# Gates of the last experts copied to 64 rows by transfers, and a second PSUM bank for the gate product

## What is computed

```
scores = sigmoid(x @ gate_w.T)
...
w_dense = zeros((T, E)).at[arange(T)[:, None], tidx].add(tw)      # E = 64 gates for each token
def body(acc, ws):
    wg, wu, wdn, cw = ws
    hmid = silu(x @ wg) * (x @ wu)                                # F = 64
    return (acc + cw[:, None] * (hmid @ wdn), None)
y, _ = scan(body, zeros_like(x), (We_gate, We_up, We_down, w_dense.T))
shared = silu(hidden_states @ Ws_gate) * (hidden_states @ Ws_up) @ Ws_down
return y + shared
```

## Time and profile before

| | |
|---|---|
| median of 3 runs | 2336.13 us (2328.97 to 2339.03) |
| the profiled execution, its time | 2336.96 us |
| its span, first to last instruction | 2334.4 us |
| TensorE matmul busy | 2067.9 us (89%) |
| VectorE busy | 1549.5 us (66%) |
| ScalarE busy | 1335.2 us (57%) |
| mean granted clock of TensorE | 0.934 |
| DMA, mean over the span | 27 GB/s |

### The profile page before, as it was taken

How to read it: one execution, slowest core, us unless ns; L and a number is a source line. 1 busy time by engine, 2 the same in 40 slices (tenths; PEclk the granted TensorE clock), 3 DMA queues, 4 the chain that set the end, 5 groups by cost and what they waited for, 6 DMA issues and landing times.

```text
span 2334.4 us, 39953 instructions
## 1 busy us (share of the span) xinstructions
PE 2067.9 (89%) x14352; PEld 1061.6 (45%) x14352; DVE 1549.5 (66%) x3792; ACT 1335.2 (57%) x2644; POOL 265.0 (11%) x355
## 2 busy tenths in 40 slices
PE   7999988799989958888888888889888888878898
PEld 3444455545556723444444444444443444434433
DVE  6767577566757776766676666667676666764554
ACT  4666644367753324676676757667675766754311
POOL 0000000144430021011010101111110101010000
PEclk9999999799999957999999989889998989979999
DMA  4000000311020010010100101010001001030000
GB/s 162 1 1 1 1 1 1 129 40 42 37 67 3 15 34 24 6 29 8 41 12 19 37 13 29 4 46 12 19 21 28 25 5 29 2 113 1 1 1 9
DMA packets 64819, 62.16 MB, mean 27 GB/s; under 512 B 8401, under 2 KB 57714, under 8 KB 63218
## 3 DMA queue, kind: packets, MB, share of 16 engines
q1 hardware_dynamic: 64626, 59.62, 8.2%
HBM read 31.28 MB, written 0.52 MB: 14 GB/s over the span
## 4 chain that ended last, share of the span: by engine, by line
PE 44%; ACT 10%; DVE 6%; issue 4%; DMA 1%; SPq 1%; ACTq 0%; DVEq 0%
PE ps L1987 7%; PE ps L1967 6%; PE ps L1947 4%; ACT big L2498 4%; PE ps L2037 3%; ACT big L2579 2%; PE ps L2139 2%; PE ps L2123 2%; DVE C_nm L2686 2%; PE ps L2239 2%; PE ps L2260 2%; PE ps L2235 2%; PE ps L1996 2%; PE ps L2160 2%; PE ps L2149 1%
## 5 line engine op out<-in xcount | busy, mean ns | idle before, releaser
L2686 DVE TENSOR_REDUCE C_nm<-ps 128x1 f32<-128x512 f32 x768 | 498.7, 684 | 216.1 <-PE ps L1947 211.8
L2498 ACT ACTIVATE big<-ps 128x512 f32<-128x512 f32 x768 | 427.3, 596 | 216.4 <-PE ps L1967 209.0
L1947 PE MATMUL ps<-C_attn 62*128 62x512 bf16 x768 | 248.1, 412 | 64.2 <-DVE C_nm L2686 48.0
L1967 PE MATMUL ps<-C_attn 64*128 64x256 bf16 x1536 | 235.7, 293 | 51.5 <-ACT big L2498 35.1
L1987 PE MATMUL ps<-big,C_attn 128*32 128x256 f32 x3072 | 227.1, 417 | 19.3 <-ACT big L2498 18.2
L1967 PEld LDWEIGHTS ps<-C_attn 64*128 64x128 bf16 x1536 | 68.5, 96 | 226.2 <-ACT big L2498 99.9
L2579 ACT ACTIVATE big<-ps,C_biasx 77x512 f32<-77x512 f32 x192 | 115.6, 679 | 68.3 <-PE ps L2127 68.2
L1947 PEld LDWEIGHTS ps<-C_attn 62*128 62x128 bf16 x768 | 60.4, 95 | 181.6 <-DVE C_nm L2686 106.1
L2432 POOL TENSOR_SCALAR lnv<-mv 128x2 f32<-128x2 f32 x72 | 16.0, 222 | 1050.1 <-DVE mv L2668 1050.1
L1987 PEld LDWEIGHTS ps<-big,C_attn 128*32 128x32 f32 x3072 | 84.5, 115 | 109.1 <-issue 46.4
L2777 DVE TENSOR_REDUCE C_nmx<-ps 128x4 f32<-128x308 f32 x192 | 78.4, 470 | 57.6 <-PE ps L2101 56.8
(11 more groups left out here) (373 smaller groups left out, 4021.7 us busy)
## 6 DMA issues: line engine op xcount, KB each, us to landing
C_attn<-C_first SPq DMA_DIRECT2D x288, 64.0 KB, 2.1
B_rot<-B_rot SPq DMA_DIRECT2D x64, 128.0 KB, 2.0
C_w<-in_C_w SPq DMA_DIRECT2D x6, 1090.0 KB, 6.0
C_attn<-in_D_ew SPq DMA_DIRECT2D x4, 1536.0 KB, 9.9
big<-in_B_ew SPq DMA_DIRECT2D x8, 514.0 KB, 9.3
normw_later<-in_norm_w SPq DMA_DIRECT2D x1, 2304.0 KB, 16.8
A_w<-in_A_w SPq DMA_DIRECT2D x2, 1024.0 KB, 9.9
A_w<-in_A_w SPq DMA_DIRECT2D x2, 768.0 KB, 11.0
```

The costliest lines, as they stand in the source:

```text
L1947: pe.matmul(ps[:, bank, :], lhsT=qs[side(hp, MAX_ROW), b, hq, t * P:(t + 1) * P], rhs=ks[side(hp, MAX_ROW), b, hq, :], start=True, stop=Tr ...
L1967: last = pe.matmul(ps[:, bank, cols(pq)], lhsT=ks[side(1 - hp, HALF), b, hq, kt * P:(kt + 1) * P], rhs=qs[side(1 - hp, HALF), b, hq, cols( ...
L2498: act.activation(prob[:, kt % 2, q2, 1 - hp, :], ps[:, bank, :], ACT.Exp, scale=SCALE)\
L2686: dve.tensor_reduce(nm[:, group % 2, t % TH, hq % 4, hp:hp + 1], ps[:, bank, :], AX.X, ALU.max, negate=True).then_inc(emptied[bank], 1)
```

## The change

The gates are no longer split and multiplied by a selector. `take_gates` copies the turned gates, 64 rows of float32, from PSUM to `d.gT` in one operation. SyncE then issues, for every pair, a transfer that reads two rows of `d.gT` and writes each 64 times, into one of three buffers of 128x512 (two in `first`, one in `hT[0]`); VectorE's second multiply reads that buffer. Transfer `j` waits for the multiply of pair `j - 3`. The second half of the weights comes in four pieces (`LATE_D`) between these transfers. The freed PSUM bank 4 becomes a second bank for the gate product.

```diff
+LATE_D = 4
...
-        for half in range(2):
-            plan["DVE"].append((at + 114 + 14 * ROUTE_PARTS + 28 * half, "split_gates", b, half))
+        plan["DVE"].append((at + 114 + 14 * ROUTE_PARTS, "take_gates", b, 0))
...
-    d.gT = flat[0:96, 2 * S:4 * S].bitcast(BF16).rearrange("p (h b s) -> p h b s", h=2, b=B)
-    d.sel = flat[0:96, 4 * S:6 * S].bitcast(BF16).rearrange("p (e d) -> p e d", d=P)
+    d.gT = flat[0:E_D, 2 * S:4 * S].rearrange("p (b s) -> p b s", b=B)
+    d.spread = flat[:, 4 * S:6 * S].rearrange("p (i s) -> p i s", i=2)
...
+        spread = (d.spread[:, 0, :], d.spread[:, 1, :], hT[0][:, :])
...
-        GATE_BANK, UP_BANK, WB_BANK, DOWN_BANK = 2, 3, PV_BANK, 1
+        GATE_BANKS, UP_BANK, DOWN_BANK = (2, PV_BANK), 3, 1
...
-                    if k:
-                        pe.wait_ge(silu_done, k)
-                    pe.matmul(ps[0:rows_d(e), GATE_BANK, :], lhsT=gate, rhs=d.hT[:, b, :], start=True, stop=True)\
+                    if k == 1:
+                        pe.wait_ge(cw_ready, UNITS * QUADS)
+                    if k >= 2:
+                        pe.wait_ge(silu_done, k - 1)
+                    pe.matmul(ps[0:rows_d(e), GATE_BANKS[k % 2], :], lhsT=gate, rhs=d.hT[:, b, :], start=True, stop=True)\
...
-                        pe.wait_ge(h_ready, k)
-                        half, pair = divmod(e - 1, PAIR_D // 2)
-                        pe.matmul(ps[:, WB_BANK, :], lhsT=d.sel[:, pair, :], rhs=d.gT[:, half, b, :],
-                                  start=True, stop=True).then_inc(wb_done, 1)
...
+                sp.wait_ge(pv_done, UNITS * 16)
+                for j in range(B * PAIR_D):
+                    b, pair = divmod(j, PAIR_D)
+                    if pair == 0:
+                        sp.wait_ge(gT_ready, b + 1)
+                    if j >= 3:
+                        before, e = divmod(j - 3, PAIR_D)
+                        sp.wait_ge(h_ready, before * STEPS_D + e + 2)
+                    sp.dma_start(spread[j % 3], d.gT[2 * pair:2 * pair + 2, b:b + 1, :].broadcast_to([2, F_D, S]))\
+                        .then_inc(spread_landed[j % 3], 16)
+                    if 2 <= j < 2 * LATE_D + 2 and j % 2 == 0:
+                        i, step_d = j // 2 - 1, PAIR_D // 2 // LATE_D
+                        part = slice(PAIR_D // 2 + i * step_d, PAIR_D // 2 + (i + 1) * step_d)
                         sp.dma_start(ew[:, part, :, :], a["D_ew"][part].rearrange("e p k d -> p e k d"))\
-                            .then_inc(d_w_loaded[b], 16)
+                            .then_inc(late_loaded[i], 16)
...
+                def take_gates(b):
                     bank = arrived(dve, ("dw", b))
...
+                    dve.tensor_copy(d.gT[:, b, :], ps[0:E_D, bank, :]).then_inc(emptied[bank], 1)
+                    drained(dve, ("dw", b))
+                    dve.sem_inc(gT_ready, 1)
...
-                            dve.wait_ge(wb_done, b * PAIR_D + e)
-                            dve.tensor_tensor(eh[:, k % 2, :], emid[:, k % 2, :], ps[:, WB_BANK, :], ALU.mult)\
+                            j = b * PAIR_D + e - 1
+                            dve.wait_ge(spread_landed[j % 3], 16 * (j // 3 + 1))
+                            dve.tensor_tensor(eh[:, k % 2, :], emid[:, k % 2, :], spread[j % 3], ALU.mult)\
                                 .then_inc(h_ready, 1)
```

More of the change, by code:

```diff
@@ L1866, in stage_c @@
         w_loaded = (w_loaded0, w_loaded1)
-        (d_small, d_w_loaded0, d_w_loaded1, dn_ready, d_order, w_ready, gT_ready, sel_set, dsel_made, gate_done, up_done,
-         wb_done, silu_done, mid_done, h_ready, down_done, acc_ready) = \
+        (d_small, d_w_loaded0, dn_ready, d_order, w_ready, gT_ready, gate_done, up_done, silu_done, mid_done, h_ready, down_done, acc_ready) = \
             (m.sem("D_" + n) for n in
-             ("small", "w_loaded0", "w_loaded1", "dn_ready", "order", "w_ready", "gT_ready", "sel_set", "sel_made",
-              "gate_done", "up_done", "wb_done", "silu_done", "mid_done", "h_ready", "down_done", "acc_ready"))
-        d_w_loaded = (d_w_loaded0, d_w_loaded1)
+             ("small", "w_loaded0", "dn_ready", "order", "w_ready", "gT_ready",
+              "gate_done", "up_done", "silu_done", "mid_done", "h_ready", "down_done", "acc_ready"))
+        late_loaded = [m.sem(f"D_late_loaded{i}") for i in range(LATE_D)]
+        spread_landed = [m.sem(f"D_spread_landed{i}") for i in range(3)]
+        spread = (d.spread[:, 0, :], d.spread[:, 1, :], hT[0][:, :])
         y_added, with_eps = m.sem("C_y_added"), m.sem("C_with_eps")
@@ L2228, in enter @@
                         drained(pe, ("dl", b))
-                    if b == 0 and e in (1, 1 + PAIR_D // 2):
-                        pe.wait_ge(d_w_loaded[e // (PAIR_D // 2)], 32)
+                    if b == 0 and e == 1:
+                        pe.wait_ge(d_w_loaded0, 32)
+                    for i in range(LATE_D):
+                        if b == 0 and e == 1 + PAIR_D // 2 + i * PAIR_D // 2 // LATE_D:
+                            pe.wait_ge(late_loaded[i], 16)
                     if e == 0:
                         drained(pe, ("dn", b))
-                    if k:
-                        pe.wait_ge(silu_done, k)
-                    pe.matmul(ps[0:rows_d(e), GATE_BANK, :], lhsT=gate, rhs=d.hT[:, b, :], start=True, stop=True)\
+                    if k == 1:
[3 more added lines that the diff above has]
+                    pe.matmul(ps[0:rows_d(e), GATE_BANKS[k % 2], :], lhsT=gate, rhs=d.hT[:, b, :], start=True, stop=True)\
                         .then_inc(gate_done, 1)
@@ L2408, in _ @@
                 sp.dma_start(d.gb, a["D_gb"].rearrange("(o e) -> o e", o=1).broadcast_to([P, E_D])).then_inc(d_small, 16)
[L2409 to L2412, removed]
+                sp.wait_ge(pv_done, (UNITS - 1) * 16)
+                for i in range(2):
+                    part = slice(i * PAIR_D // 4, (i + 1) * PAIR_D // 4)
+                    sp.dma_start(ew[:, part, :, :], a["D_ew"][part].rearrange("e p k d -> p e k d"))\
+                        .then_inc(d_w_loaded0, 16)
+                sp.wait_ge(pv_done, UNITS * 16)
[11 more added lines that the diff above has]
+                        part = slice(PAIR_D // 2 + i * step_d, PAIR_D // 2 + (i + 1) * step_d)
                         sp.dma_start(ew[:, part, :, :], a["D_ew"][part].rearrange("e p k d -> p e k d"))\
-                            .then_inc(d_w_loaded[b], 16)
+                            .then_inc(late_loaded[i], 16)
             @block.gpsimd
@@ L2469, in spread_heads @@
                             .then_inc(sel_made, 1)
[L2471 to L2481, removed]
                 for _, n, s in timeline(GPSIMD):
-                    if n == UNITS - 1 and s in GPSIMD[n % B]["VX"]:
-                        spread_gates()
                     step(n, s)
@@ L2868, in route @@
                         dve.tensor_scalar(d.wd, d.wd, 2.5, None, ALU.mult).then_inc(w_ready, 1)
-                def split_gates(b, half):
+                def take_gates(b):
                     bank = arrived(dve, ("dw", b))
[L2872 to L2880, removed]
-                    cd.after(dve.tensor_copy(gT[32:64, :], d.rem[0:32, :]))
-                    cd.after(dve.tensor_copy(d.rem[32:64, :], d.rem[0:32, :]))
-                    ins = dve.tensor_tensor(gT[64:96, :], d.rem[32:64, :], gT[32:64, :], ALU.subtract)
-                    if half == 0:
-                        cd.after(ins)
-                    else:
-                        ins.then_inc(gT_ready, 1)
+                    dve.tensor_copy(d.gT[:, b, :], ps[0:E_D, bank, :]).then_inc(emptied[bank], 1)
+                    drained(dve, ("dw", b))
+                    dve.sem_inc(gT_ready, 1)
                 def expert(k):
```

17 lines of the change are left out of this document (4 added, 13 removed).

## The result

The changed kernel takes **2641.93 us** (median of four runs, 2621.76 to 2654.95) beside 2333.35 us for the kernel before on the same chip: 1.1313 times as long, 95% interval 1.1236 to 1.139. Forecast were 2784 us and 2460 to 2840 us. Direction and cause were right; the mean time of a transfer was set too high.

The account below looks back on a forecast made before the run. TensorE bound the second batch before; afterwards the transfers would. Gates ready at 2088.1, first packet 2089.6, 64 x 10.5 = 672.0, weights 8.6, tail 10.8: span 2781.0, plus 2.6 around it, 2784 us; range 2460 to 2840 us.

Parts of the forecast that it names:

- krow's 16 KB: Earlier transfer, two neighbouring SBUF rows each copied to 8 places: 0.65 us, 25 GB/s, taken as model for gate transfers.
- T = 10.5 us for all 64: Time each gate transfer occupies its engines in the expert loop: 256 KB at krow's rate, 64 times, 672.0 us.
- the new transfer reads two neighbouring rows, so krow's is the nearest: Step choosing krow's transfer to price each gate transfer in the expert loop: 10.5 us.
- The bounds of 8.6 to 11.2 us: Limits on one gate transfer: 8.6 us by the one-row copy's 30 GB/s, 11.2 us counting krow's last packet.
- the case that got 73%: Gate transfers limited by their source rows at 8.6 to 11.2 us each: 2662 to 2829 us, likeliest 2784; chance 73%.
- two engines with less or no disturbance: Gate transfers at 5.6 to 8.6 us each: 2470 to 2662 us; chance 16%.
- The first rival: Two engines of a gate transfer don't disturb each other: 5.6 us each, 2470 us; within the 16% case.
- Weights between the transfers: Four pieces of late weights between gate transfers, 32 packets on each of the two engines: 8.6 us added.
- Hidden transfers: Rival: gate transfers spread over all engines land before the multiply wants them: 17 us saved, 2320 us; chance 4%.
- No overlap: Rival: every gate transfer pays 2 us of start and landing: 2912 us; chance 7%, shared with transfers slower than 11.2 us.
- Clock: TensorE a quarter to half busy, granted clock near 0.5; tail after the last multiply 10.8 us instead of 9.4.
- The gate bank: Second PSUM bank lets gate(k) start before Silu(k-1) has read, but up(k) still waits for step k-1's product: worth little.

Follow-up runs that it names:

- e2: Changed kernel with each transfer reading two gate rows 4 apart instead of neighbours, still two engines: 2441.42 us, 1.045 times the kernel before.
- e3: Changed kernel with each transfer reading two gate rows 32 apart instead of neighbours, still two engines: 2731.1 us, 1.169 times the kernel before.
- e6: Changed kernel with every transfer reading gate rows 0 and 1: 2763.83 us, 1.1833 times the kernel before.
- e9: Changed kernel with one buffer instead of three, each transfer issued behind the multiply of the pair before: 2892.6 us, 1.2369 times the kernel before.
- e1: Changed kernel with each gate row copied by a transfer of its own, on 16 engines instead of 2: 2615.68 us, 1.1196 times the kernel before.
- e4: Against e1, gates of a batch written once to HBM and each row read from there: 2310.62 us, 0.9885 times the kernel before.

## Why the prediction was right, and where its size was off

*Direction, place, cause: right.* Two engines, limited by the two source rows, at 25 GB/s: the small packets (4 notes in 2240 to 2260, in which two transfers ended), the share of 0.12 and the first steps of 10.1 to 10.6 us are the forecast's. krow's 16 KB were the right row, for the right reason: e2 and e3 changed only the rows that are read, and the step went to 5.37 and 10.01 us.

*The term that was mis-sized: T = 10.5 us for all 64.* From copied gates to the end the forecast was 12.0 + 63 x 10.5 + 8.6 + 10.8 = 692.9 us; measured were 12.1 (2062.71 to 2074.84), 534.1 and 10.8 (2608.90 to 2619.7). So the loop came out 670.1 - 534.1 = 136 us shorter. The profiled execution lies 162 us under 2784; nearly all of the rest are the 25.4 us by which it reached the gates earlier, which is no merit or fault of the sum. The run that always reads the same two rows splits it: its loop took 653.3 us (2089.55 to 2742.88). So 16.8 us are the price of an undrifted transfer (10.3 instead of 10.5) and of the weights, and 119.2 us are the drift. krow's transfer, eight packets to each engine, shows no such change: the step "the new transfer reads two neighbouring rows, so krow's is the nearest" priced a single transfer rightly and took it for a constant over a queue of them. The bounds of 8.6 to 11.2 us just missed the mean of 8.48, for a reason that they did not contain. So by its own conditions the result lies outside the case that got 73% (2662 to 2829 us) and in the stretch from 5.6 to 8.6 us, which belonged to two engines with less or no disturbance (16%); the stated range holds it because that case was taken in, not because the drift was seen.

*The first rival, two undisturbed engines at 5.6 us,* is no other case but the second phase of the same one: its rate appears at each change of rows, for longer each time, until the step there is 5.3 us. As a kernel of its own (e2) it took 2441 us, where 2470 were forecast: 64 packets an engine in 5.27 us are 82 ns each, for the 88 ns that the earlier trace rows gave with all sixteen engines at work, not with one alone.

*Weights between the transfers:* 8.6 us forecast; in the run with the same rows always, the first ten steps, in which they load, took 105.2 us (2089.55 to 2194.77), and ten at the mean of the other 53 would take 103.4: about 2 us. Why so little was not tried.

*Hidden transfers:* out of reach for this source in every form that was tried, but right as a price: the forecast said 2320 us, 17 us under the profiled 2337 of before; with HBM as the source it is 20 us under the kernel before in the longest series (2311.96 against 2332.22), 27 in the first (2310.62 against 2337.32).

*No overlap:* 2912 us forecast at 2 us a transfer; with one buffer 2892.6 us and 2.3 us. The three buffers do what they were counted for, and they are also what lets the drift grow. From issue to landing a transfer took 28 us early in the loop and 19 at its end, where about 30 were forecast.

*Clock:* forecast near 0.5 with TensorE a quarter to a half busy; granted were 0.73 to 0.81 at 52 to 68%, and 0.50 only in the tail, where the sum used it and the tail came out at the forecast 10.8 us. In the loop it was no part of the sum. The row that the prediction took for low load, 2076 to 2080, has TensorE busy 2.51 of 4.00 us: it shows the level, not that low load brings it. *The gate bank* "is worth little": right.

## What to carry to other kernels

Price a copy inside SBUF by the rows that it reads, not by its bytes alone: many copies of a few neighbouring rows share one way out. Sixteen engines for two hardly widened it (8.08 us a step beside 8.48), and three buffers for one didn't as long as the group of rows stayed the same (256 KB in 10.3 us, 25 GB/s, in e6; 25 to 29 GB/s in e9). If rows have to be copied out many times over, one trip through HBM and reads that use all engines took this loop from 8.48 us a step to 3.35, where nothing waits for the transfers any more. And compare a step's price with a series, not with one transfer: where two engines share a source, a queue can move them apart.

## What was not expected of the hardware

- The two engines of a transfer don't stay together. At each change of the group of rows one gets a little farther ahead: once the weights have landed, the step there shrinks by 0.19 us from one change to the next in the changed kernel ((8.75 - 5.35) / 18, steps 11 to 47), by 0.21 with rows 32 apart ((9.90 - 7.35) / 12) and by 0.20 in the other order ((9.13 - 5.54) / 18). The gain needs the change of rows (e6) and queued transfers (e9). The lead itself needs only the queue: in e6 it grows without a change of rows, by 0.017 us a transfer ((1.11 - 0.06) / 62), while with one buffer it is 0.04 to 0.08 us throughout. Why a change of rows makes it grow so much faster stays open.
- Busy DMA engines may only be waiting: 86% of 16 engines for 32 GB/s (e1), 33.5% for 105 GB/s with HBM as the source (e4, DMA view of 2240 to 2260):

```profile
DMA packets 1281, 2.11 MB, mean 105 GB/s; under 512 B 256, under 2 KB 256, under 8 KB 1280
...
q1 hardware_dynamic: 1280, 2.10, 33.5%
```

- An issue on SyncE can take 10.07 us for one transfer (that of a piece of the weights, above) when the queue is full, beside the 0.75 us of the earlier trace rows.
